# Token rows of an expert stage turned by DMA instead of TensorE, with the attention pipeline reordered around it

## What is computed

```python
x = x + _linear_attention(_layernorm(x), Wq, bq, Wk, bk, Wv, bv, Wo, bo)
x = x + _moe_forward(_layernorm(x), router_w, w1, b1, w2, b2)

# attention: q, k = elu(.) + 1; per token
s = s + einsum('bhd,bhm->bhdm', k_i, v_i); z = z + k_i
out_i = einsum('bhd,bhdm->bhm', q_i, s) / (einsum('bhd,bhd->bh', q_i, z) + 1e-6)

# experts: softmax over the two best of 8 router logits
hmid = gelu(einsum('th,efh->etf', x, w1) + b1)
y = einsum('etf,ehf->eth', hmid, w2) + b2
out = einsum('eth,te->th', y, combine)
```

## Time and profile before

| | |
|---|---|
| median of 3 runs | 1096.58 us (1094.77 to 1099.1) |
| profiled execution | 1091.56 us, span 1089.8 us, mean granted TensorE clock 0.963 |
| busy, whole span | PE 951.3 us (87%), DVE 831.0 (76%), ACT 660.6 (61%), POOL 699.4 (64%) |
| attention stage | until about 647 us |
| expert stage | from about 669 us to the end |
| HBM | read 72.01 MB, written 67.44 MB |

### The profile page before, as it was taken

How to read it: one execution, slowest core, us unless ns; L and a number is a source line. 1 busy time by engine, 2 the same in 40 slices (tenths; PEclk the granted TensorE clock), 3 DMA queues, 4 the chain that set the end, 5 groups by cost and what they waited for, 6 DMA issues and landing times. The chain is left out here.

```text
span 1089.8 us, 33554 instructions
## 1 busy us (share of the span) xinstructions
PE 951.3 (87%) x10092; PEld 784.3 (72%) x10093; DVE 831.0 (76%) x2201; ACT 660.6 (61%) x1253; POOL 699.4 (64%) x606
## 2 busy tenths in 40 slices
PE   4599888988898898888889833999999999999995
PEld 2377667766766775675677733999999999999994
DVE  5378999998997997997999874666666666666663
ACT  5667776776776677666767432555555555555552
POOL 5626677786677678776778553556556565566555
PEclk9799999999998999998999966999999999999998
DMA  3665886446654654673655282455555555555554
GB/s 111 149 142 125 274 178 156 126 153 161 165 126 137 159 132 135 155 173 98 164 139 139 89 316 97 89 90 96 96 96 88 87 98 96 97 85 95 92 97 49
DMA packets 129125, 140.30 MB, mean 129 GB/s; under 512 B 12512, under 2 KB 122208, under 8 KB 128416
## 3 DMA queue, kind: packets, MB, share of 16 engines
q1 hardware_dynamic: 101184, 102.38, 38.0%
q0 software_dynamic: 26688, 35.93, 17.8%
q10 hardware_dynamic: 1184, 1.18, 0.3%
HBM read 72.01 MB, written 67.44 MB: 128 GB/s over the span
## 5 line engine op out<-in xcount | busy, mean ns | idle before, releaser
L1497 POOL DMA_INDIRECT out<-yt,to_token x142 | 225.7, 1589 | 172.8 <-DVE yt L1360 108.6
L792 ACT ACTIVATE ahl<-pS 128x512 f16<-128x512 f32 x240 | 141.0, 599 | 74.7 <-PE pS L508 73.1
L1035 DVE SCALAR_TENSOR_TENSOR ahl<-pS,ahl 128x512 f16<-128x512 f32 x240 | 161.2, 682 | 28.8 <-ACT ahl L792 27.5
L1414 POOL DMA_INDIRECT expert_in<-xn,cur x128 | 130.5, 1020 | 35.1 <-issue 33.1
L960 ACT ACTIVATE g<-pS,b1s 128x256 f32<-128x256 f32 x144 | 60.2, 470 | 90.7 <-PE pS L433 90.7
L433 PE MATMUL pF<-xT,was 128*128 128x512 f16 x384 | 102.7, 410 | 11.8 <-DVE xT L1040 11.8
L505 PE MATMUL pS<-cbs 128*128 128x512 bf16 x240 | 93.0, 387 | 20.2 <-DVE ahl L1035 12.2
L1331 DVE TENSOR_TENSOR ghl<-g,ghl 128x1024 f16<-128x1024 f32 x71 | 87.1, 1227 | 24.3 <-ACT ghl L982 24.3
L433 PE MATMUL pU<-w2s,ghl 128*128 x864 | 100.5, 273 | 1.9 <-DVE ghl L1331 1.9
L433 PE MATMUL pS<-gT,w1s 128*128 128x256 f16 x864 | 101.1, 274 | 0.1
L433 PE MATMUL pF<-w2s,ghl 128*128 x840 | 97.4, 273 | 0.0
(11 more groups left out here) (160 smaller groups left out, 2323.9 us busy)
## 6 DMA issues: line engine op xcount, KB each, us to landing
xg<-expert_in SPq DMA_DIRECT2D x71, 260.0 KB, 3.0
qk_parts<-qkhl SPq DMA_DIRECT2D x32, 512.0 KB, 2.9
qst<-qk_parts SPq DMA_DIRECT2D x96, 128.0 KB
kst<-qk_parts SPq DMA_DIRECT2D x48, 256.0 KB
xs<-x SPq DMA_DIRECT2D x16, 512.0 KB, 4.6
xr<-x SPq DMA_DIRECT2D x16, 512.0 KB, 4.8
out<-x SPq DMA_DIRECT2D x16, 512.0 KB, 3.2
expert_in<-pads SPq DMA_DIRECT2D x16, 260.0 KB, 3.7
```

What stands on the lines that cost most here:

```text
L792: nc.scalar.activation(ahl[:, b % 2, 0, n * 4 * C:(n + 1) * 4 * C], score_bank(fr, n)[:], ACT.Relu).then_inc(sc_hi, 1)
L1035: V.scalar_tensor_tensor(ahl[:, b % 2, 1, cols], score_bank(fr, n)[:], 0.0, ahl[:, b % 2, 0, cols], ALU.max, ALU.subtract).then_inc(sc_lo, 1)
L1414: G.indirect_dma_start(xg_dram, bass.IndirectOffsetOnAxis(ap=cur[:, qp, 2 * b + t:2 * b + t + 1], axis=0), xn2[:, qp, b], None).then_inc(s ...
L1497: G.indirect_dma_start(out, bass.IndirectOffsetOnAxis(ap=to_token[:, c % 2, s:s + 1], axis=0), yt[:, c % 2, s], None, compute_op=ALU.add). ...
```

## The change

It has four parts.

1. **Rows as f16 pairs, turned by DMA.** In the attention stage the row that is scattered is now the f16 high part and the f16 residue of the normalised x1 side by side, the same 1024 bytes. In the expert stage SP loads a tile with a transposing DMA straight into gT (both parts), and the four numbers of each row with a second DMA into `about`. There are four buffers instead of two, and the loop holds four tiles. `turn`, and the splitting by ScalarE and VectorE, are gone.
2. **Second norm by ScalarE.** `norm2_apply` becomes an activation with a scale and a shift (`norm2_shift`, VectorE, one operation on 4 numbers), in place in x1. It waits for the output DMA of x1. ScalarE writes the f16 high parts (`rows_high`, 2 per step), VectorE the residues (`rows_low`, 2 per step).
3. **The gap's exponent by ScalarE.** exp(second - first) is now one activation per b, with the second logit as bias and scale -1; VectorE's `pd` is gone.
4. **Order.** x of the next step is transposed and split in the last third of a body. With it projections, values, norm 1, rstd, v_low and w1_high move in the fixed orders of the engines, and scores of step 0 use two banks instead of four.

```diff
-        gT = sb("gT", [P, 2, 2, KC * MT], F16, moe)
+        about = sb("about", [P, BUFS, 2, ROW - D], F32, moe)
+        gT = sb("gT", [P, BUFS, 2, KC, MT], F16, moe)
...
+        rows = data[:].bitcast(F16)
...
-                if c >= 2:
-
-                    sp.wait_ge(gt_ps, t - 1)
-                    sp.wait_ge(meta, t - 1)
-                sp.dma_start(xg[:, c % 2], xg_dram[bass.ds(row, MT), :].rearrange("(s p) d -> p s d", p=P)).then_inc(xg_in[c % 2], 16)
+                if c >= BUFS or not isinstance(j, int):
+
+                    sp.wait_ge(h_ps, 2 * t - 2 * BUFS + 2)
+                    carry_wait(sp)
+                    sp.wait_ge(meta, t - BUFS + 1)
+                    carry_wait(sp)
+                sp.dma_start_transpose(gT[:, c % BUFS].rearrange("p a k n -> p (a k) n"),
+                                       xg_dram[bass.ds(row, MT), 0:D].bitcast(F16)).then_inc(gT_in[c % BUFS], 16)
+                sp.dma_start(about[:, c % BUFS],
+                             xg_dram[bass.ds(row, MT), D:ROW].rearrange("(s p) d -> p s d", p=P)).then_inc(about_in[c % BUFS], 16)
...
-                    pe.wait_ge(gt_lo, t + 2)
+                    pe.wait_ge(gT_in[p4], 16 * ((c + 1) // BUFS + 1) + 16 * j)
...
+                def norm2_apply(n):
+                    if n == 0:
+                        act.wait_ge(ln2_sh, r + 1)
+
+                        act.wait_ge(x1_out, 16 * r + 16)
+                    for b in (2 * n, 2 * n + 1):
+                        nc.scalar.activation(x1[:, b], x1[:, b], ACT.Identity, bias=sh2[:, b:b + 1],
+                                             scale=rs2[:, b:b + 1]).then_inc(xn2_done, 1)
+
+                def rows_high(n):
+                    act.wait_ge(xn2_done, 4 * r + 2 * n + 2)
+                    if c >= 4 and n == 0:
+
+                        act.wait_ge(scat_out[c % 2], 128 * rh)
+                    nc.scalar.activation(rows[:, c % 2, 2 * n:2 * n + 2, 0:D], x1[:, 2 * n:2 * n + 2], ACT.Copy).then_inc(rows_hi, 1)
...
-                    act.wait_ge(top_gap, q + 1)
-                    nc.scalar.activation(one_exp[:, :, 1], pd[:, 0], ACT.Exp).then_inc(top_exp, 1)
+                    act.wait_ge(top_gap, 4 * q + 4)
+                    for b in range(B):
+                        nc.scalar.activation(one_exp[:, b, 1:2], mx[:, b, 0:1], ACT.Exp, bias=mx[:, b, 1:2],
+                                             scale=-1.0).then_inc(top_exp, 1)
...
-                    V.scalar_tensor_tensor(xn2[:, rp, b, 0:D], x1[:, b], mv2[:, b, 0:1], rs2[:, b:b + 1].to_broadcast([P, D]),
-                                           ALU.subtract, ALU.mult).then_inc(xn2_done, 1)
+                    V.scalar_tensor_tensor(sh2[:], mv2[:, :, 0], -1.0, rs2[:], ALU.mult, ALU.mult).then_inc(ln2_sh, 1)
+
+                def rows_low(n):
+                    dve.wait_ge(rows_hi, 2 * r + n + 1)
+                    V.scalar_tensor_tensor(rows[:, rp, 2 * n:2 * n + 2, D:2 * D], x1[:, 2 * n:2 * n + 2], 1.0,
+                                           rows[:, rp, 2 * n:2 * n + 2, 0:D], ALU.mult, ALU.subtract).then_inc(rows_lo, 1)
...
-                if fr:
-                    x_transposes(0)
-                    x_transposes(1)
+                if c == 0:
+                    x_transposes(0, 0)
+                    x_transposes(0, 1)
...
+                if turn_next:
+                    x_transposes(i + 1, 0)
                 if bk:
                     scores(2, 3)
                     out_project(s, 1)
+                if turn_next:
+                    x_transposes(i + 1, 1)
```

More of the change, by code:

```diff
@@ L294, in tiles @@
                 body(0, c)
-            with engine.Fori(0, (NT - 5) // 2) as j:
-                for c in (2, 3):
+            with engine.Fori(0, LOOPS) as j:
+                for c in range(2, 2 + BUFS):
                     body(j, c)
-            for c in range(2 + (NT - 5) // 2 * 2, NT):
+            for c in range(2 + LOOPS * BUFS, NT):
                 body(0, c)
@@ L923, in body @@
                     score_hi(3, 1)
[L925 to L927 removed]
+                if fr and c != 1 or c == 1 and not front:
+                    v_high()
                 if bk:
@@ L1454, in body @@
                     scatter(2)
+                if fr and c != 1 or c == 1 and not front:
+                    v_low()
                 if bk:
```

346 lines of the change are left out of this document (169 added, 177 removed).

## The result

The changed kernel takes 1165.45 us (median of 4 runs, 1161.13 to 1165.94), the kernel before 1095.67 beside it: ratio 1.0626, 95% interval 1.0587 to 1.0665. I had forecast 1054.

The account below looks back on a forecast made before the run. VectorE was taken as nearest to the bound in the attention stage, TensorE as the bound in the expert stage. -30.8 - 2 - 10 = -43 us gave a median of 1054 us, range 1027 to 1086.

Parts of the forecast that it names:

- Expert stage, -30.8: Expert stage: TensorE's four transposes a tile go, 0.44 us of 5.67 over 70 tiles, -30.8 us.
- Transposing DMA at nothing: Expert tile load: the transposing DMA costs nothing, covered by idle DMA time.
- my bounds of 1.05 and 3.1: Expert tile's DMA: 1.05 us if it moves like the plain load; 3.1 us is the room left in 5.23.
- Rival B: Expert stage: transposing DMA becomes the bound of each of 71 tiles; 0.11 slower, 0.02 still faster.
- First tile, -2: Start of expert stage: transposes, copy and residue replaced by a DMA, -2 us, range 0 to -2.7.
- The lists of the engines: Attention step: summed work per engine, VectorE from 33.9 to 32.4 us, ScalarE from 26.2 to 30.5 us.
- The stretch that I had put at 18.5 us for ScalarE: First half of an attention step: ScalarE works 18.5 us without a gap, before 16.4 us with one gap of 1.40.
- The step, -0.7 us: Attention step: 18.5 + 0.5 + 18.1 = 37.1 us, so -0.7 us a step, -10 us over fourteen steps.
- What I named as exposed: Attention step: last head group's `out_transpose` behind two projections, VectorE's `out_lo` waiting for ScalarE's copy; nothing added.
- An edit at nothing that was not nothing: Attention step: ScalarE's new wait for the output DMA costs nothing, most of ScalarE's 18.5 us stand ahead of it.
- Rival A: Attention step: ScalarE becomes the bound, +1.5 us a step, 1084 us; 0.13 still faster, 0.07 no change, 0.02 slower.
- My own sign for it, steps over 38.5 us: Attention stage: steps over 38.5 us would show that ScalarE had become the bound.

Follow-up runs that it names:

- the second transposing DMA of a tile: Changed kernel with each expert tile's rows transposed by DMA twice, the second time into a buffer nobody reads: 1202.71 us.
- out_early: Changed kernel with VectorE's lower half of score (0,2) ahead of norm 1's statistics, and the fourth head block's out transposition and copy earlier: 1202.91 us.
- the filled step: Changed kernel with 12 useless TensorE multiplies a step, 8 before scores(1,0) and 4 before attend(0): 1147.53 us.
- new_order_norm_vector: Changed kernel with the second norm and the logit gap back on VectorE, new order kept: 1124.76 us.
- shifted_once: Changed kernel with 8 useless TensorE multiplies once before step 1, repeated steps untouched: 1195.86 us.
- old_order_norm_vector: Changed kernel with the attention stage in the old order, second norm (in place) and gap exponent on VectorE; f16 rows and transposing DMA kept: 1123.78 us.
- start_vector: Changed kernel with project(3) before attend(0), fourth head block's out transposition and scores (0,2), (0,3) earlier, second norm and logit gap on VectorE: 1102.64 us.
- after: The changed kernel itself, all four parts of the change, against the kernel before: 1165.45 us, ratio 1.0626.
- start_scalar: Changed kernel with project(3) before attend(0), fourth head block's out transposition and scores (0,2), (0,3) earlier; second norm and exponents stay on ScalarE: 1122.17 us.
- project3_first: Changed kernel with one edit on TensorE, project(3) ahead of attend(0): 1121.99 us.

## Why the prediction was wrong

**Expert stage, -30.8: right, it gave -26.5.** The tile is 5.24 us (forecast 5.23). Over 70 tiles of 5.24 that leaves 3.3 us: 0.8 lie in the first two tiles, and most of the rest in every fourth tile from the eighth on, which takes 5.3 to 5.6 us, as often as the loop of four tiles turns. The chain through gelu stayed covered.

**Transposing DMA at nothing: right.** By the shares of q1 (48.3% of 1194.4 us less 38.0% of 1164.1, over 71) the second transposing DMA of a tile takes 1.9 us of the 16 engines, between my bounds of 1.05 and 3.1. The first, with the small DMA beside it, adds less: 38.0% of 1164.1 less 38.0% of 1089.8 is 28 us, 0.4 a tile more than the plain load. The Trainium skill has it as fast as a regular DMA (Advanced Engine Details and Errata, X-Bar Transpose); by these two figures it is 1.4 to 1.8 times the plain load, which itself is only estimated at 1.05, and it didn't matter. The other page's 1309 ns a piece, eight in a row, is not what a tile of 256x512 costs. Rival B was empty.

**First tile, -2.** From the end of the last scatter to the first hidden layer it was 7.0 us and is 5.6: -1.4, within 0 to -2.7.

**The lists of the engines: right, or too dear.** ScalarE is busy 245.2 / 364 x 44.4 = 29.9 us a step (forecast 30.5), VectorE 30.2 (forecast 32.4). The stretch that I had put at 18.5 us for ScalarE, from its first kn copy to the end of the read of score (2,0), is this window of one step, with the columns of the earlier trace rows; below it is the line of ScalarE's timeline with the longest wait in it.

```profile
386.84:410.90 24.06, 17.80 (x142) 11.73 (x141) 14.89 (x48) 18.09 (x40) 11.13 (x10) 0.79 0.43 99
```

```profile
402.05 0.60 ACT L798 ACTIVATE ahl<-pS 128x512 f16<-128x512 f32 x1 [5.96 <-PE pS L529]
```

ScalarE's work in it is 18.1 us, nearly the forecast, but the stretch takes 24.1: the forecast said "without a gap", and there is one of 5.96 us in which ScalarE waits for TensorE, which is at half clock.

**The step, -0.7 us: wrong by 7.3 us, and this is nearly the whole miss** (14 steps of 7.3 are 102 of the 111 us between 1054 and 1165.5). The first half is 24.1 us instead of 18.5, the rest of the step 20.3 instead of 18.6. It came from two sentences: the step is the longer list of each half, and "For such late hand-overs I add nothing, since ScalarE's stretch is counted in full". Of TensorE the sum has only 0.5 us of k transposes, though it is the engine with the most work after VectorE (33.1 us of 37.8), and it has no term for TensorE's waits and the half clock that these traces show behind them (10.2 us a step; the kernel before had 17 us in the whole stretch). What I named as exposed, `out_transpose` behind two projections and `out_lo` behind ScalarE's copy, is the 1.84 us that VectorE waits at 433.90. I priced it at nothing. In the trace TensorE's wait of 2.23 us follows from it, though taking it away (out_early) only moved the wait. Of the 7.6 us by which the step is longer than an undisturbed one of before (36.8), the filled step gives back 3.8 with the clock (and 10.2 us of half clock at the 2.3 for 6.8 of new_order_norm_vector are 3.5), and the old order with its norm on VectorE shows 2.1 for the rows' halves and the norm in place. The other 1.7 are not assigned, and all of these shares are subject to what shifted_once shows. Neither list that I had summed is the bound: VectorE's 30.2 and ScalarE's 29.9 us stand in a step of 44.4.

**An edit at nothing that was not nothing.** I covered the new wait for x1's output DMA with ScalarE's list ahead of it. Inside the steps that is right: between 206 and 570 us no engine waits for it. At the end of the stage there is no list, and TensorE stands for 11.8 us; old_order_norm_vector, which has the same wait, loses 7.9 us there. The two score banks of step 1, also at nothing, may be the 5.5 us of that step in the old order; no run separates them.

**Rival A was the right name with the wrong mechanism.** "ScalarE becomes the bound", beyond +2.4 us a step no gain: the step grew 6.6 over the old mean of 37.8. ScalarE's added work did cost 40.3 us up to the experts in the new order, but ScalarE isn't full: it is late at two places, with the copy of aT and with the scaling of x1 (1.79 us of TensorE's time in every step). My own sign for it, steps over 38.5 us, came true. Its price of 1.5 and the chance of 0.02 for slower were the error: I took the price from the length of a list, where these runs say that it counts which engine waits for the late piece. That ScalarE's share differs from 11 to 74 us between orders, no list could have told.

What stays open: how the 98 us divide further. Rows 54.1, order 3.6, norm and exponents 40.3 add up along one path through the versions, but shifted_once takes 29 us more up to the experts with the repeated steps untouched, and start_vector with the four exponents alone 57.

## What to carry to other kernels

In a pipeline where three engines hand each other small pieces in a fixed order, don't take the step as the longest list: follow TensorE's waits and what the granted clock does behind each. Put work that is ready ahead of such a wait (one moved projection: -43 us), since removing one wait may only uncover the next, longer one. Before believing a small edit in such a kernel, run a control that shifts the start and changes nothing else: here such a control came out 30 us apart. Run the version without the shift again beside it; that was left out here, and so the cause of the 30 us stays open.

## What the runs showed of the hardware that I had not expected

- The same repeated instructions ran in two patterns, 44.4 us, or 45.7 and 46.4 in turn, each exact to 0.1 us over ten steps (after and shifted_once). What decides between them is not shown.
- At turns of the loop VectorE stood for 2.3 to 5.1 us, waiting for nothing that the profile shows, in most versions and not at all in start_vector, new_order_norm_vector and shifted_once, with the same loop. Written out without the loop, three kernels lost these stands. The Trainium skill (Advanced Engine Details and Errata, Control Flow Timing) gives some 0.05 to 0.11 us for a branch; the rows show twenty times that and more.
- Half clock doesn't simply add: 6.8 us of it cost 2.3, start_scalar had twice that of project3_first in steps of the same 40.9 us, and start_vector, nearly as much as start_scalar, has steps of 38.9 and 39.6.
